# Dividing eight PSUM banks between side jobs and row maxima in a fused hybrid block: three side banks and two maximum banks instead of two and three

## What is computed

```python
x = x + attn_a(layernorm(x))   # one causal softmax over -distance/4 for all 16 heads
x = x + ffn(layernorm(x))      # sigmoid(xr Wr^T) * (relu(xk Wk^T)^2 Wv^T), xr/xk mix x with the token before
x = x + attn_b(layernorm(x))   # 16 heads of 16, softmax(q k^T / 4), causal
x = x + ffn(layernorm(x))
```

## Time and profile before

| quantity | value |
|---|---|
| median of 3 runs | 2311.16 us (2307.39 to 2319.46) |
| profiled execution, its own time | 2316.06 us |
| its span in the trace | 2314.3 us |
| mean granted TensorE clock | 0.92 of full |
| TensorE busy | 1929.1 us (83%) |
| VectorE busy | 1417.5 us (61%) |
| ScalarE busy | 1254.3 us (54%) |
| GpSimd busy | 1024.2 us (44%) |
| DMA | 97.27 MB, 18.6% of 16 engines |

### The profile page before, as it was taken

How to read it: one execution, slowest core, us unless ns; L and a number is a source line. 1 busy time by engine, 2 the same in 40 slices (tenths; PEclk the granted TensorE clock), 3 DMA queues, 4 the chain that set the end, 5 groups by cost and what they waited for, 6 DMA issues and landing times. The chain is left out here.

```text
span 2314.3 us, 32515 instructions
## 1 busy us (share of the span) xinstructions
PE 1929.1 (83%) x9842; PEld 936.3 (40%) x9842; DVE 1417.5 (61%) x4173; ACT 1254.3 (54%) x2673; POOL 1024.2 (44%) x1074
## 2 busy tenths in 40 slices
PE   4477888888988899788987889888887889988986
PEld 3344343334433354324543345333443335432423
DVE  2336677567676666666765666756656666677642
ACT  0623654675537555394545755366554855555563
POOL 4454354335642455334743266423654246422414
PEclk8677899989998899989999899998999899999998
DMA  3006011310132111211122011231113111141100
GB/s 96 0 20 117 1 28 42 69 28 15 43 85 34 28 29 53 67 29 28 33 67 64 13 29 37 76 63 28 28 37 83 28 28 28 43 87 29 29 19 19
DMA packets 64347, 97.27 MB, mean 42 GB/s; under 512 B 15655, under 2 KB 58029, under 8 KB 58030
## 3 DMA queue, kind: packets, MB, share of 16 engines
q1 hardware_dynamic: 64174, 95.20, 18.6%
HBM read 61.09 MB, written 33.55 MB: 41 GB/s over the span
## 5 line engine op out<-in xcount | busy, mean ns | idle before, releaser
L852 ACT ACTIVATE pt<-exp_bank 128x512 f32<-128x512 f32 (+3 forms) x1536 | 742.5, 494 | 806.5 <-PE exp_bank L822 797.0
L867 DVE CUSTOM_DVE_ANT_0 max_bank<-max_bank,mask 128x128 f32<-128x128 f32 (+3 forms) x1024 | 500.3, 502 | 495.2 <-PE max_bank L811 478.2
L822 PE MATMUL exp_bank<-qs,ks 98*128 98x512 bf16 (+3 forms) x1536 | 523.8, 347 | 72.5 <-ACT pt L852 66.3
L811 PE MATMUL max_bank<-ks,qs 96*128 96x512 bf16 (+3 forms) x1536 | 525.0, 349 | 24.3 <-DVE piece_max L870 17.2
L870 DVE TENSOR_REDUCE piece_max<-max_bank 128x1 f32<-128x512 f32 x512 | 342.9, 686 | 164.7 <-PE max_bank L811 161.5
L837 PE MATMUL o_bank<-pt,v 128*17 128x512 f32 (+3 forms) x3072 | 346.2, 525 | 8.0 <-ACT pt L852 3.0
L889 POOL TENSOR_SCALAR_AFFINE_SELECT pt<-pt 128x512 f32<-128x512 f32 x256 | 170.1, 664 | 404.2 <-ACT pt L852 403.8
L353 POOL TENSOR_SCALAR xh<-xs,mv,rstd 128x256 f32<-128x256 f32 x256 | 322.6, 1266 | 10.0 <-PE side L379 3.8
L822 PEld LDWEIGHTS exp_bank<-qs,ks 98*128 98x128 bf16 x1536 | 153.9, 101 | 353.4 <-ACT pt L852 229.5
L811 PEld LDWEIGHTS max_bank<-ks,qs 96*128 96x128 bf16 x1536 | 154.7, 101 | 257.9 <-issue 102.1
L544 PE MATMUL side<-vp,p 128*128 128x260 f32 x576 | 185.2, 450 | 33.7 <-ACT p L473 18.3
(11 more groups left out here) (94 smaller groups left out, 2243.0 us busy)
## 6 DMA issues: line engine op xcount, KB each, us to landing
parts_dram<-parts SPq DMA_DIRECT2D x64, 384.0 KB, 2.6
qs<-parts_dram SPq DMA_DIRECT2D x192, 128.0 KB, 7.0
ks<-parts_dram SPq DMA_DIRECT2D x32, 384.0 KB, 4.8
xs<-in_L_attn_a_x_dram SPq DMA_DIRECT2D x16, 512.0 KB, 4.3
ks<-parts_dram SPq DMA_DIRECT2D x32, 256.0 KB, 5.5
out_dram<-xs SPq DMA_DIRECT2D x16, 512.0 KB, 3.1
ks<-parts_dram SPq DMA_DIRECT2D x32, 128.0 KB, 5.9
qs<-neg_maxT SPq DMA_DIRECT2D x64, 8.0 KB, 1.9
```

The lines of the kernel that those rows point to most:

```text
L811: pe.matmul(max_bank[u % MAX_BANKS][:, 0:k1 - k0], qs[r][0:KROWS, j, P * tile:P * (tile + 1)], ks[r][0:KROWS, j, k0:k1], start=True, stop= ...
L822: pe.matmul(exp_bank[k % EXP_BANKS][:, 0:q1 - q0], ks[r][:, j, P * kt:P * (kt + 1)], qs[r][:, j, q0:q1], start=True, stop=True).then_inc(s ...
L852: act.activation(pt[:, e % 2, j, 0:q1 - q0], exp_bank[k % EXP_BANKS][:, 0:q1 - q0], ACT.Exp, scale=SCALE).then_inc(exp_done, 1)
L867: dve.tensor_tensor_reduce(scores, scores, mask[:, HALF - w:HALF], 1.0, LOWEST, ALU.add, ALU.max, piece_max[:, j, m:m + 1]).then_inc(max_f ...
```

## The change

One maximum bank becomes a side bank. The number of exponential banks (two) and the output bank stay, so all eight banks are in use before and after. The planner is given three places in `free`, so that jobs wait less often for a planned bank and the rule "the bank planned to be free first" now chooses among three.

```diff
-MAX_BANKS, EXP_BANKS = 3, 2
+MAX_BANKS, EXP_BANKS = 2, 2
@@ place()
-    free, before, shift, u = [BEGIN, BEGIN], BEGIN, 0, BEGIN
+    free, before, shift, u = [BEGIN, BEGIN, BEGIN], BEGIN, 0, BEGIN
@@ bass_hybrid()
-        side = [psum(f"side{k}") for k in range(2)]
+        side = [psum(f"side{k}") for k in range(3)]
@@
-        emptied = [None, None]
+        emptied = [None, None, None]
```

## The result

The changed kernel takes **2161.72 us** (median of 4 runs, 2155.86 to 2164.97) against 2311.69 us for the one before: ratio 0.9345, interval 0.9313 to 0.9377. The profiled execution has a span of 2154.1 us.

What follows compares the result with a forecast made beforehand. TensorE, stopped mostly by side-bank waits, bounds the kernel. -77 + 46 = -31 us takes the profiled 2316.06 us to 2285; that execution lies 4.9 us above the median, so 2280 us is forecast, range 2238 to 2320.

Steps and rivals of the forecast that it cites:

- What bounds the kernel: TensorE, busy 1929.1 of 2314.3 us, sets the pace; side-bank waits of 149 us against 17 for maximum banks.
- Part 1, the third side bank: TensorE's waits for side-bank readers shrink with one more bank: 77 us gained, lower end 40, upper end 107.
- 107 us of waiting go: Side-bank waits: 132 us in 227 jobs counted to the bank's release, of which 25 us in 24 jobs remain.
- the 30 us taken off: Bank waits in and just behind projection stretches where VectorE is full, some 30 us over eight sequences, not gained.
- Part 2, the lost maximum bank: Maximum matmuls (L811) must wait for the reader two quarters back: 46 us lost, lower end 20, upper end 160.
- the hidden part: Share of the 66 us of maximum-matmul delay lying behind ScalarE in the distance stage, costing no time: 20 us.
- The moved order: 195 side jobs start one to three quarters earlier, covered by idle time of VectorE, ScalarE and GpSimd: cost nothing.
- The change of name: Rival: side-bank waits become waits for data and exponential banks, so no change; about 2311 us, chance 0.17 including clock.
- Starving: Rival: in attention with 512-wide maxima, two maximum banks let VectorE run dry; +53 us, 2364 us, chance 0.11.
- The clock: Rival case of TensorE's granted clock, grouped with waits only changing name: about 2311 us, chance 0.17 together.
- What I said would show it: Profile after: bank waits under 60 us, L811 60 to 90, exponential waits 55 to 90, TensorE busy 84 or 85%.
- One sign: Most of the 60 to 90 us of waits at L811 would lie in stretches like 1608 to 1623 us.

Runs made afterwards that it cites:

- the version with the old order: Changed kernel with every instruction in the plan order of the kernel before, a third side bank given out afterwards: 2150.33 us, ratio 0.9298 to the kernel before.
- the pair that differs in nothing else: Two versions in the plan order of the kernel before, both with two maximum banks, one with two side banks, one with three: 2331.87 and 2150.33 us.
- the run with the loss alone: Kernel before with two maximum banks instead of three, still two side banks, one bank idle: 2331.87 us, ratio 1.0082 to the kernel before.
- the control: Kernel before with the maximum matmul issued twice in quarters 96 to 127 of each sequence: 2334.63 us, ratio 1.0096 to the kernel before.

## Why the prediction was wrong

**What bounds the kernel: right.** TensorE set the pace, and its waits for side banks were the part to be had. With all but a few us of them gone, and by these waits alone, the time falls by 182 us. One reading in the timeline was off by a job: with two side banks the value job at 1504.54 takes the bank of the one before last, so the reader at 1504.07 empties the job of this row, and not the one at 1502.06:

```profile
1500.67 1.11 PE L516 MATMUL side<-wvp,xt 128*128 128x259 f32 x4 [0.34 <-DVE v L743]
```

The step that it explains, TensorE held until VectorE has caught up, stands.

**Part 1, the third side bank: the term that failed.** The step was "107 us of waiting go ... I take these off and leave 77 us". The measured value of that term is 182 us. It was too small in three ways. First, 107 was 132 less 25. The 132 stop at the release of the bank, though the time from a release to the next start is lost as well (the table had 149). The 25, for 24 jobs that would still find their bank full, hardly came: one such row, 1.6 us, is left in the version with the old order. The gaps fell by 135 us in the pair that differs in nothing else. Second, the 30 us taken off because "TensorE cannot gain where VectorE is full" were not lost: the quarters where values and projections lie shrank from 75.5 to 59.7 us and kept 0.8 us of gaps. A window of the old order with three side banks in these projections, against the earlier trace rows:

```profile
1350.00:1365.00 15.00, 15.00 (x73) 6.97 (x72) 14.75 (x42) 7.13 (x14) 8.61 (x9) 1.00 0.24 81
```

VectorE is as full as there (14.75 us) and TensorE is busy for all 15.00 us. Over the 59.7 us VectorE is busy for 49.7, so it has time to catch up. Third, there was no term for TensorE's busy time, which fell by 50 us in that pair. Part of it is the end of a matmul that no longer lies bare before a wait; in the stretch at the full clock that alone makes 15.8 us of time out of 13.7 of gaps. The other part is the clock, which was at its lower level for 48 us less. As a whole it was 182 us of time for 135 us of gaps.

**Part 2, the lost maximum bank: right in kind, twice too large.** 46 us were forecast and 21 measured. The new idle time at L811 is 41 us in the run with the loss alone (66 in 192 places by my count), and against it stand 23 us less of waits of the exponential scores and of L644. I had put the hidden part at 20 us and into the distance stage alone.

**The moved order: costed at nothing, measured at +11 us.** The cover I named, the idle time of the other engines, was there. What I left out is that jobs which start earlier can meet waits for data and readers that they did not meet before: some 4 us of them in quarters 144 to 191 of a sequence. Why the clock stays up in the first 32 quarters of most sequences, which gives nearly as much back, no run shows.

**The sum by the runs:** +21 (maximum bank), -182 (side bank), +11 (order), which is -150.

**The rivals.** The change of name was small: waits for data rose by 20 us (L379 behind GpSimd by 8, L732 by 5, L910 by 4, L516 by 3) and one fell by 10 (L644). Starving did not happen at two banks; at one the waits at L811 are far above the 107 us that I had named. The clock, which shares a chance of 0.17 with the change of name, did not fall: it rose, from 0.92 to 0.941, and at a quarter of a us for each us at the lower level that is some 30 of the 150 us, an estimate. In the values and projections it stood at 0.99 and there was little to win, but the first 32 quarters, in the distance stage, went from 0.74 to 1.00, and the forecast has no term for a rise.

**What I said would show it** mostly did: bank waits under 60 us (about 13), L811 at 60 to 90 (77.2), exponential scores at 55 to 90 (67.0), VectorE's idle time before its maxima down from 640 to 490 us. The busy share is 86% where I said 84 or 85. One sign failed: the waits at L811 are not mostly in the stretch with 512-wide maxima and statistics. A full sequence has 3.1 to 3.8 us of them in its first 32 quarters and 2.3 to 2.9 in quarters 64 to 95. These bounds were wide: bank waits of about 13 us are far below what a gain of 77 us would have left.

## What to carry to other kernels

Look at how far an engine must have caught up when a wait ends, not only at how long the wait is. Here a bank whose reader stood behind newer work in its queue forced the two engines into step (1.01 us idle for TensorE at 1504.54 in the earlier trace rows), and one more bank there was worth almost nine times what it cost where the queue is already two deep (182 us against 21). Price a wait of TensorE above its idle time: in these runs 1.16 times where the clock did not change, 1.35 to 1.45 times over whole runs, in which the time at the lower clock level moved too. And give a plan's resources and its order separate runs: here the extra bank was worth 182 us and the order that the planner made of it took 11 back.

## What the runs showed of the hardware that was not expected

Time at TensorE's lower clock level cost half of what the missing share would give. The same 32 quarters took 33.0 us at the full clock and 36.4 with about 13.8 us at the lower level, a quarter of a us for each. In a stretch where ScalarE is busy 31 of 33 us that is no contradiction: TensorE runs slower but is not alone in setting the pace. The fastest version of all has the lower clock of the two candidates, 0.92.

By the missing share, half of 111 us, some 55 us, would have come back when doubled matmuls took the old order with three side banks from a mean clock of 0.921 to 0.947. The version became 6 us slower, and if the added matmuls cost the 24 us of the control, 18 came back.

A maximum matmul issued twice cost 0.11 us on average in quarters 96 to 127, where 512-wide ones start 0.22 us apart in the timeline. Some of them are narrower, and some of their time fell into waits that were there already; the two were not separated.
